# The last chunk of 36 experts' gate-up weights kept on chip, and an expert's loads issued when the first half of an earlier expert's outputs has landed

## What is computed

```python
def _L0_ffn_ref(hidden_states, gate_weight, gate_up_proj, down_proj, old_to_new):
    ...
    logits = x @ gate_weight.T
    logits = jnp.where(old_to_new[None, :] == -1, -jnp.inf, logits)
    probs = jax.nn.softmax(logits.astype(jnp.float32), axis=-1).astype(logits.dtype)
    top_v, top_i = jax.lax.top_k(probs, TOP_K)
    ...
    gu = jnp.einsum('ech,eoh->eco', xb, gate_up_proj)
    g, u = jnp.split(gu, 2, axis=-1)
    h = jax.nn.silu(g) * u
    out = jnp.einsum('eci,ehi->ech', h, down_proj)
    ...
    final = jnp.zeros_like(x).at[tok].add(y * w[:, None])

x = x + _L0_attn_ref(_layernorm(x, axis=-1), ...)
x = x + _L0_xattn_ref(_layernorm(x, axis=-1), ctx_2048, mask_BxS2_bk0)
x = x + _L0_ffn_ref(_layernorm(x, axis=-1), ...)
```

## Time and profile before

| | us |
|---|---|
| median of 3 runs (1121.84 to 1123.8) | 1121.9 |
| the profiled execution | 1131.94 |
| its span, first to last instruction | 1130.2 |
| TensorE busy | 1042.7 |
| VectorE busy | 864.6 |
| ScalarE busy | 621.7 |
| GpSimd busy | 570.6 |
| granted TensorE clock, mean | 0.978 |

### The profile page before, as it was taken

How to read it: one execution, slowest core, us unless ns; L and a number is a source line. 1 busy time by engine, 2 the same in 40 slices (tenths; PEclk the granted TensorE clock), 3 DMA queues, 4 the chain that set the end, 5 groups by cost and what they waited for, 6 DMA issues and landing times.

```text
span 1130.2 us, 24509 instructions
## 1 busy us (share of the span) xinstructions
PE 1042.7 (92%) x6564; PEld 835.2 (74%) x6564; DVE 864.6 (77%) x2382; ACT 621.7 (55%) x1751; POOL 570.6 (50%) x529
## 2 busy tenths in 40 slices
PE   5998899999999999999999987999999999999992
PEld 4776777777777777777777775788777877778771
DVE  5776788878878888888788865387787778787871
ACT  4554445555455455554554542376666667666661
POOL 2114565665666566656656566434444434444343
PEclk9999899999999999999999998899999999999995
DMA  7999474543312113112122120399999999999974
GB/s 294 373 286 289 155 256 156 196 150 119 135 53 91 50 47 93 47 47 92 47 75 65 39 76 11 111 237 248 249 251 245 249 260 243 254 247 260 247 179 55
DMA packets 94052, 185.72 MB, mean 164 GB/s; under 512 B 24791, under 2 KB 24791, under 8 KB 93504
## 3 DMA queue, kind: packets, MB, share of 16 engines
q1 hardware_dynamic: 62640, 145.10, 40.8%
q0 software_dynamic: 31376, 40.20, 17.1%
HBM read 116.00 MB, written 122.00 MB: 211 GB/s over the span
## 4 chain that ended last, share of the span: by engine, by line
PE 48%; DMA 26%; issue 12%; POOL 6%; ACT 4%; DVE 3%; another core or an unknown queue 0%; POOLq 0%; SPq 0%; DVEq 0%; ACTq 0%
DMA layer_out<-qk_both,slot_table 24%; PE ps L1181 23%; PE ps L1166 9%; PE ps L1171 5%; PE ps L1208 3%; POOL layer_out L619 2%; PE ps L1279 2%; PE ps L1312 2%; POOL slot_records L543 2%; ACT heads_t L642 1%; ACT heads_high L640 1%; PE ps L1188 1%; PE ps L1296 1%; DMA gu_sb<-in_weights 1%; PE ps L1337 1%
## 5 line engine op out<-in xcount | busy, mean ns | idle before, releaser
L543 POOL DMA_INDIRECT slot_records<-row,slot_idx x256 | 266.4, 1041 | 90.1 <-issue 60.4
L619 POOL DMA_INDIRECT layer_out<-qk_both,slot_table x96 | 163.3, 1701 | 234.3 <-DMA layer_out<-qk_both,slot_table 204.1
L554 POOL TENSOR_TENSOR rstd<-mv,neg_half 128x1 f32<-128x1 f32 x96 | 79.5, 828 | 132.2 <-DVE mv L914 78.8
L640 ACT ACTIVATE xn_t<-ps 128x512 f32<-128x512 f32 x64 | 38.3, 598 | 138.9 <-PE ps L1166 109.7
L1181 PE MATMUL ps<-w_high,xn_high 128*128 128x512 f32 x384 | 114.1, 419 | 0.7 <-ACT xn_high L640 0.7
L1337 PE MATMUL ps<-w_high 128*128 128x192 f32 x576 | 91.2, 280 | 19.5 <-DVE w_low L1088 17.5
L1181 PE MATMUL ps<-w_low,xn_high 128*128 128x512 f32 x384 | 108.5, 405 | 0.0
L1181 PE MATMUL ps<-w_high,xn_low 128*128 128x512 f32 x384 | 107.2, 401 | 0.0
L1337 PEld LDWEIGHTS ps<-w_high 128*128 128x128 f32 x576 | 76.4, 192 | 40.0 <-issue 39.3
L675 ACT ACTIVATE probs<-ps,neg_max_s 128x128 f32<-128x128 f32 x256 | 89.8, 377 | 19.4 <-DVE neg_max_s L911 19.4
L1088 DVE TENSOR_TENSOR w_low<-gu_sb,w_high 128x1536 fp32r<-128x1536 f32 x48 | 84.4, 1757 | 11.9 <-ACT w_high L640 9.1
(11 more groups left out here) (164 smaller groups left out, 2431.4 us busy)
## 6 DMA issues: line engine op xcount, KB each, us to landing
gu_sb<-in_gate_up SPq DMA_DIRECT2D x48, 768.0 KB
slot_records<-dn_both SPq DMA_DIRECT2D x6, 3366.0 KB, 20.7
w_raw<-slot_records SPq DMA_DIRECT2D x48, 280.5 KB
dn_both<-in_down_proj SPq DMA_DIRECT2D x48, 256.0 KB
x_ln<-in_x SPq DMA_DIRECT2D x32, 256.0 KB
x_res<-in_x SPq DMA_DIRECT2D x32, 256.0 KB
ctx_t_sb<-in_ctx_t SPq DMA_DIRECT2D x32, 256.0 KB
ctx_sb<-in_ctx_rows SPq DMA_DIRECT2D x32, 256.0 KB
```

Of the source, the lines that this page charges most:

```text
L543: pool.indirect_dma_start(out=records, out_offset=bass.IndirectOffsetOnAxis(ap=slot_idx[:, s.parity, k:k + 1], axis=0), in_=row[:, s.parit ...
L554: pool.tensor_tensor(rstd[:, :], mv[:, 1:2], neg_half[:, 0:1], ALU.pow).then_inc(steps.sem, 1)
L619: pool.indirect_dma_start(out=out, out_offset=bass.IndirectOffsetOnAxis(ap=slot_table[0:PART[h], 2 * d.index + h:2 * d.index + h + 1], axi ...
L640: act.activation(dst, src, ACT.Copy).then_inc(steps.sem, 1)
```

## The change

The last of the four gate-up chunks (384 of 1536 columns, 196.6 kB an expert) of experts 2 to 37 is loaded once, into buffers of the batch phase that are free by then, in four transfers of 8, 12, 8 and 8 experts, by SyncE behind the last batches. For these experts `load_gate_up` moves three chunks (589.8 kB). For the 12 others the last chunk is a second DMA. The host lays the last chunks out as one array. To make room the buffers of the batch phase are cut from three larger ones (`project_bufs`, `attend_bufs`, `cross_bufs`).

The loads of the expert phase are written out. From expert 0 on SyncE waits until the first half of the outputs of expert n has landed, and then issues rows(n+4), gate-up(n+5) and down(n+3). `d_add` becomes one semaphore for each half and parity; ScalarE's `y0` waits for the first half alone, VectorE's `y1` for the second, GpSimd for both. Cast and difference of the gate-up weights are two instructions each, of 1152 and 384 columns. The expert turns of ScalarE and VectorE are written out; TensorE keeps its loop.

```diff
+        project_bufs = sb("project_bufs", [P, 6 * DM])
+        attend_bufs = sb("attend_bufs", [P, 9 * DM])
+        cross_bufs = sb("cross_bufs", [P, 12 * DM])
...
+        KEPT = [(project_bufs, 0, 8), (attend_bufs, 0, 12), (cross_bufs, 0, 8), (cross_bufs, 8, 8)]
+        KEPT_FROM = 2
...
-        d_add = [sem("outputs_added0"), sem("outputs_added1")]
+        d_add = [[sem(f"outputs_of_half{h}_added{n}") for n in range(2)] for h in range(2)]
...
+        def written_out(turn):
+            for n in range(2 * EPAIRS):
+                turn({k: Batch(n // 2, n % 2 - s, E) for k, s in ESKEW.items()})
...
-                sp.dma_start(gu_sb[:, e.parity, :, :], gate_up[bass.ds(e.index * P, P), :, :])\
+                sp.dma_start(gu_sb[:, e.parity, 0:KC - 1, :], gate_up[e.index * P:(e.index + 1) * P, :, :])\
                   .then_inc(d_gu[e.parity], 16)
+                if e.index not in kept_at:
+                    sp.dma_start(gu_sb[:, e.parity, KC - 1, :], gate_up_last[:, e.index, :])\
+                      .then_inc(d_gu[e.parity], 16)
+
+            def load_kept(group):
+
+                bufs, at, n = KEPT[group]
+                first = min(e for e, (g, _) in kept_at.items() if g == group)
+                sp.dma_start(bufs[:, at * GU:(at + n) * GU].rearrange("p (e n) -> p e n", n=GU),
+                             gate_up_last[:, first:first + n, :]).then_inc(d_kept[group], 16)
...
+                if b["attend"].is_(NB):
+                    sp.wait_ge(att_t.sem, att_t.after(b["attend"].back(1), "pv"))
+                    load_kept(1)
+                if b["cross"].is_(NB):
+                    sp.wait_ge(crs_t.sem, crs_t.after(b["cross"].back(1), "scores"))
+                    load_kept(2)
+                    sp.wait_ge(crs_t.sem, crs_t.after(b["cross"].back(1), "readout"))
+                    load_kept(3)
...
+                if b["project"].is_(NB):
+                    sp.wait_ge(prj_t.sem, prj_t.after(b["project"].back(1), "kT"))
+                    load_kept(0)
...
-            load_gate_up(Batch(1, 0, E))
-            with sp.Fori(1, E // 2 - 1) as pair:
-                for off in range(2):
-                    load_rows(Batch(pair, off, E))
-                    load_gate_up(Batch(pair, off + 1, E))
-                    load_down(Batch(pair, off, E))
...
+            load_gate_up(expert(2))
+            load_rows(expert(2))
+            load_gate_up(expert(3))
+            load_down(expert(2))
+            load_rows(expert(3))
+            load_gate_up(expert(4))
+            for n in range(E - 3):
+
+                sp.wait_ge(d_add[0][n % 2], moved(expert(n), 1))
+                if n + 4 < E:
+                    load_rows(expert(n + 4))
+                if n + 5 < E:
+                    load_gate_up(expert(n + 5))
+                load_down(expert(n + 3))
...
                 if d.back(1).exists():
-                    pool.wait_ge(d_add[d.back(1).parity], moved(d.back(1), 2))
+                    pool.wait_ge(d_add[1][d.back(1).parity], moved(d.back(1), 1))
+                    pool.wait_ge(d_add[0][d.back(1).parity], moved(d.back(1), 1))
...
-                    act.wait_ge(d_gu[t.parity], moved(t, 1))
+                    act.wait_ge(d_gu[t.parity], gate_up_moved(t))
+                    if t.index in kept_at:
+                        act.wait_ge(d_kept[kept_at[t.index][0]], 16)
...
-                    copy(gu_high[:, t.parity, :, :], gu_sb[:, t.parity, :, :], wgu_a)
+                    act.activation(gu_high[:, t.parity, 0:KC - 1, :], gu_sb[:, t.parity, 0:KC - 1, :], ACT.Copy)
+                    copy(gu_high[:, t.parity, KC - 1, :], last_chunk(t), wgu_a)
...
-                        act.wait_ge(d_add[d.back(2).parity], moved(d.back(2), 2))
+                        act.wait_ge(d_add[0][d.back(2).parity], moved(d.back(2), 1))
...
-            expert_turns(act, expert_turn)
+            written_out(expert_turn)
...
-                    left_by(gu_low[:, t.parity, :, :], gu_sb[:, t.parity, :, :],
-                            gu_high[:, t.parity, :, :]).then_inc(wgu_v.sem, 1)
+                    left_by(gu_low[:, t.parity, 0:KC - 1, :], gu_sb[:, t.parity, 0:KC - 1, :],
+                            gu_high[:, t.parity, 0:KC - 1, :])
+                    left_by(gu_low[:, t.parity, KC - 1, :], last_chunk(t),
+                            gu_high[:, t.parity, KC - 1, :]).then_inc(wgu_v.sem, 1)
...
-                        dve.wait_ge(d_add[d.back(2).parity], moved(d.back(2), 2))
+                        dve.wait_ge(d_add[1][d.back(2).parity], moved(d.back(2), 1))
...
-            expert_turns(dve, expert_turn)
+            written_out(expert_turn)
```

69 lines of the change are left out of this document (41 added, 28 removed).

## The result

The change made the kernel slower. The median went from 1122.34 us (1121.84 to 1123.8, four runs) to 1192.01 us (1188.02 to 1196.34, four runs): a ratio of 1.062 (95% interval 1.0577 to 1.0662). The forecast was 1096 with a range of 1084 to 1115, so both the sign and the range were wrong. The profiled execution took 1194.04 us, its span was 1192.3 (before: 1130.2).

The account below looks back on a forecast made before the run. It took the once-per-expert add loop (8.03 us), with DMA at share 0.99 and TensorE near at 7.34, as the bound. Savings 22.8 + 3.2 + 0.35 - 0.5 = 25.9 us gave 1106 profiled, 1096 median; range 1084 to 1115.

Parts of the forecast that it names:

- (a): Expert loads: 197 kB less for experts 2 to 37 cuts the DMA's loaded price from 8.1 to 7.5 us an expert.
- (b): SyncE's gate: halves land 1.2 us apart instead of 3.0; first half takes 5.5 to 6 us, setting the add loop.
- burst rows: Profile rows at 742 to 760 us: first halves of experts 1 and 2 took 6.9 and 7.4 us among back-to-back loads.
- (c): Gate-up cast and difference split in two: 0.16 us per further instruction, hidden; 7 us if that cover were gone.
- (d): Written-out loops on ScalarE, VectorE and SyncE: register instructions go, programs lengthen; taken as 0, bounds -2 to +2 us.
- (e): y0 and y1 waiting on one half each: GpSimd still waits for both, loop keeps its length; 0.
- (f): Loading 7.1 MB of kept chunks behind the last batches: costs 0 to 2 us, taken as 0.5.
- later than 740 us: Start of expert phase: expert 0's add coming after this time was a sign of the prediction being wrong altogether.
- The sum: Expert phase: kept experts at 7.5 us, the other ten 7.8; 25.9 us saved in all, median 1096.
- D: Rival, add loop: sharing with loads makes first halves 6.9 us, period 8.4, 9 us lost, 1131; chance 0.10.
- C: Rival, add loop: first half at 6.5 us among loads, period 8.0, 8 us saved, 1114; chance 0.22.
- B: Rival, TensorE alone binds: all periods 7.34 us, 36 us saved, 1086; chance 0.18.

Follow-up runs that it names:

- e10: Changed kernel, SyncE's loads let go by a GpSimd memset marker behind both adds instead of the first half's landing: ratio 1.001 to the kernel before.
- e12: Kernel before with loads let go by a memset marker behind both adds, SyncE's loads written out, all bytes loaded, no split copies: ratio 1.002.
- e14: e8 with each gate-up load also waiting for VectorE's low part of the rows two experts before: ratio 1.013 to the kernel before.
- e15: e6, all bytes loaded, with each gate-up load also waiting for VectorE's low part of the rows two experts before: ratio 1.016.
- e19: e12 with every load issued one expert earlier: median 1119.69 us of six executions; ratio 0.987 on the three shorter, 0.997 on all six.
- e4: Changed kernel, gate kept, moving one gate-up chunk instead of three for experts 2 to 47, 0.39 MB less per set: ratio 0.997 to the kernel before.
- e9: Kernel before with only ScalarE's and VectorE's expert loops written out, SyncE keeping its loop: ratio 1.002.
- e6: Kernel before with the loops of ScalarE, VectorE and SyncE's loads written out, nothing else: ratio 1.019.
- e11: Kernel before with only a semaphore for each half, ScalarE's y0 and VectorE's y1 each waiting for their own half: ratio 1.101.
- e1: Changed kernel without the gate, SyncE's loads in the old order as buffers come free: 1225.06 us, ratio 1.095 to the kernel before.
- e8: e1 with y0 and y1 waiting for both halves again, kept chunks and split copies staying: ratio 1.010 to the kernel before.
- e18: e10 with every load issued one expert earlier, kept chunks staying: 1118.27 us, ratio 0.995 to the kernel before.
- e7: Changed kernel, SyncE's loads waiting for a bare GpSimd semaphore increment behind both adds instead of the first half's landing: ratio 1.052 to the kernel before.

## Why the prediction was wrong, point by point

**What bounds the kernel.** The loop was read rightly: an expert's second half lands, 0.27 us, the next first half, 1.86 us. It is still the loop after. The reading of the DMA share as a second bound was wrong. At 0.99 the queues were full of work *in flight*, and their work could be cut by a tenth without effect (e10 and e12, e14 and e15) or done at 258 instead of 249 GB/s (e19's profiled execution).

**(a) Fewer bytes: the price failed.** 8.1 to 7.5 us was taken from a share of busy time per megabyte (the sum as written gives 7.4). In e10 against e12 it is 0.2 us of period and nothing in the time. Inside the lockstep e4 makes a megabyte worth 4.2 us, but the changed kernel's last ten periods, with all bytes, are only 0.09 us longer than those with a kept chunk.

**(b) The gate: the step that failed.** The loop was written as 1.2 + 0.27 + the first half's latency, and it is the loop that runs: 0.70 + 0.32 + 8.60 = 9.62. What was mis-sized is the last term, 5.5 to 6 us predicted, 8.60 measured. The first term is near for the wrong reason. It was worked out as 1.85 + 4.2 - 4.9, and is 1.98 + 7.32 - 8.60. The loads' data was to move after the second half was down in its light-load 4.2 us; it moved ahead of it, and the second half took 7.32. Both latencies were mis-sized by some 3 us, and their difference hid it. The error was to take's 4.9 us "under full load" as the price of a first half among loads. At 882.53 the engines were full, but with loads of which the last had been issued 2.8 us before; the next one went out 2.57 us later, when the first half was half through (timeline of before, SyncE's issues around that add):

```profile
879.70 0.42 SPq L404 DMA_DIRECT2D gu_sb<-in_gate_up  x1
885.10 0.33 SPq L410 DMA_DIRECT2D dn_both<-in_down_proj  x1
```

So that row shows a first half with no load issued near its start. The two burst rows, 6.9 and 7.4, were the nearest to what the gate does at every expert, and the row was chosen against them.

**(c) Split copies: held.** They sit on no chain: e10, which has them, is at 1.001, and e12, which has not, at 1.002.

**(d) Written-out loops: half held.** ScalarE's and VectorE's cost nothing (e9). SyncE's cost 1.9% (e6), some 21 us, outside the bounds of -2 to +2 us. It is no cost of longer programs (e12 at 1.002 has it too): the issues came closer together, and the rows 0.6 us nearer to the adds. The bound was set for the engine's own time; the trigger it pulls was not looked at.

**(e) Half waits: 0 predicted, 10% alone (e11).** The working looked only at who is held by the wait. It did not ask what the earlier `y0` lets go: ScalarE's next casts, VectorE's split, the free down buffer, and down's load 0.6 us earlier, ahead of the second add. In the changed kernel the gate sets the issue times, so this cost should not add to the gate's (no run has the gate with both waits); it is what remained when e1 took the gate away, as e8 shows.

**(f) Kept chunk loads: held.** Expert 0's add starts at 740.51 (before 739.92), 0.6 us later for the 0.5 forecast. That it is "later than 740 us", one of the signs of being wrong altogether, was a bound that its own term already broke. The burst's disappearance was right too: 7.64 us between experts 1 and 2.

**The sum.** 42 periods of 7.5 were predicted. From expert 5 to 43 alone, 38 periods came out 1.59 us longer than before instead of some 0.5 shorter: +60.4 us. Experts 43 to 47 add 5.7, expert 0's add 0.6, and the start gives 4.6 back: 62.1.

**The rivals.** D had the sign and the place, a first half delayed by loads around it, and was under-sized (6.9 us and 8.4, measured 8.60 and 9.62): it doubled two thirds of the adds' engine time, while in fact both adds land only when the whole set is through. The Trainium skill (DMA: Bandwidth & Descriptors, Queues, rings and completion order) says that an engine takes turns between its queues packet by packet. The sign agrees (8.60 us), but D's even sharing from the start is not what the trace shows: from 905 to 909 us the load queue had 82.5% of the engines and the add queue 1.8%. C's argument, that a period of 8.0 would leave the DMA idle and therefore could not be, was the same error as in (a): the engines stand empty for about 2 us of every period, since the next set waits for a landing. B's 7.34 was not reached by any run over a long stretch; the best is 7.65 from expert 5 to 33 in e18, and e19's ten periods after it, 7.51.

**What stays open.** Why the packets of an add that is issued among loads start so late: 4.8 us after the add, where a set of 1.4 MB was issued around it. Whether that is the order in which queues are served or the making of the add's own transfers was not tried. Why GpSimd's add instruction takes up to 2.5 us instead of 1.55 in some kernels (means of the first add: 2.18 in e11, 1.92 in e10, 1.89 in e1); it helps to put down ahead of the second add. And why e19's executions fall into two groups 1.5% apart.

## What to carry to other kernels

Where a chain runs through a DMA's latency, look up when other transfers are *issued* relative to it, and keep the loads from going out ahead of it. Here every kernel with a full set of loads ahead of the second add had over 9.3 us a period, and 0.7 us behind it was enough for 8.0; the mean DMA share says neither that bytes bound the kernel nor that a latency under load is known. Taking a wait or a register instruction away from an engine that leads to an issue moves that issue, and 0.6 us was worth 2 to 10% here. A gate that starts many transfers at one landing makes a lockstep with idle engines: a gate on the issue of the chain's own transfer took the loss back (e10, 1.001), and one item deeper it gained half a per cent (e18, 0.995).

## What the runs showed that was not expected

- An indirect add of 64 rows (0.13 MB) lands 4.2 us after its issue with no loads about, 5.4 to 5.5 with loads from 1.6 us after it on, 5.9 to 6.1 with the first at +0.7, 6.4 at +0.7 with the rows close behind, and 7.2 to 8.1 with the first load of 1.4 to 1.6 MB ahead of it. With 1.07 MB ahead of it (e4) it is 5.5.
- In the changed kernel the packets of a first half's add begin 4.8 us after it (2.2 before), while the loads' queue moves 0.82 MB in 4 us.
- Taking waits away from two engines made the kernel 10% slower (e11), and putting them back, 8% faster (e8 against e1).
- A semaphore increment placed behind an indirect DMA on GpSimd let the loads go only 0.1 us behind the landing that the engine waits for next (e7); a memset there let them go about 3.6 us after the first add's start (e10).
- Five issues on SyncE take 3.3 us in the hardware loop with register addresses and 2.6 us written out with constants.
- The granted clock of TensorE was 0.90 in the expert window after (1.00 before), where TensorE was busy for 318.1 of 365.6 us, and 1.00 again in e18, where it was busy for 287.1 of 296.9. GpSimd's adds followed the landings within 0.32 us in the mean there, so none of the loss is put down to TensorE.
